# A gated recurrence stage, unrolled and skewed by one block over three engines

## The reference, cut to what matters

```python
h = layernorm(x)                      # rows of x, eps 1e-5
q, k, v, g = h @ Wq, h @ Wk, h @ Wv, h @ Wg
a = (h @ Wa)[:, :256] + 1j * (h @ Wa)[:, 256:]
a = sigmoid(abs(a)) * exp(1j * angle(a))
state[t] = a[t] * state[t - 1] + k[t] * v[t]   # complex, from 0 in each sequence
y = q * state                          # complex
y = groupnorm(y) * silu(g)             # groups of 8 channels, statistics over the sequence
```

## Time and profile before

| | |
|---|---|
| three runs, us | 3324.5, 3325.3, 3327.1; median 3325.3 |
| the profiled execution, us | 3331.5 |
| its span, us | 3329.7 |
| busy over the span | TensorE 80%, VectorE 59%, ScalarE 32%, GpSimd 41% |
| the stage that is changed | 0 to 395.5 us of the span |
| VectorE busy in it, us | 361.3 |
| granted clock of TensorE in it | 0.75 of 2.4 GHz; 0.90 from 620 us on |

### The profile page before, as it was taken

The page is one execution under the profiler, slowest core; times in us unless marked ns, Lnnn a source line. Parts: engine busy times, 40 slices in busy tenths (PEclk is TensorE's granted clock), DMA queues, the critical chain, the costliest instruction groups (busy, mean ns, idle before and its releaser), DMA issues. The chain is left out here.

```text
span 3329.7 us, 36467 instructions
## 1 busy us (share of the span) xinstructions
PE 2674.7 (80%) x12202; PEld 1820.2 (55%) x12202; DVE 1977.3 (59%) x3556; ACT 1053.3 (32%) x1637; POOL 1380.7 (41%) x865
## 2 busy tenths in 40 slices
PE   6555389956899999997477987879779676997998
PEld 2222156645799999996133433434334233665997
DVE  8999868645122222222788888999889894332111
ACT  4544222200111111111345545455454430221111
POOL 0000034426333333332058687686786852112332
PEclk8777699965899999998688998999889887998999
DMA  3000100011899999986200000101001000115996
GB/s 109 0 0 0 43 7 19 13 31 30 297 328 323 323 328 326 318 310 219 103 26 26 30 34 26 39 26 39 26 26 38 26 26 22 36 42 202 349 349 235
DMA packets 90565, 395.04 MB, mean 119 GB/s; under 512 B 20854, under 2 KB 48006, under 8 KB 63840
## 3 DMA queue, kind: packets, MB, share of 16 engines
q1 hardware_dynamic: 68864, 351.46, 30.0%
q0 software_dynamic: 21600, 42.37, 3.6%
HBM read 364.94 MB, written 39.29 MB: 121 GB/s over the span
## 5 line engine op out<-in xcount | busy, mean ns | idle before, releaser
L1240 POOL TENSOR_TENSOR ss_h<-ss_h,ss_cs 128x2048 f32<-128x2048 f32 x128 | 578.9, 4524 | 84.4 <-DVE ss_h L1603 76.6
L1320 PE MATMUL ss_y<-ss_h,all_ident 128*128 128x512 f32 x1024 | 528.3, 665 | 39.0 <-POOL ss_h L1240 39.0
L1095 DVE TENSOR_TENSOR experts_in<-experts_sil,experts_pU 128x512 f32<-128x512 f32 x176 | 121.0, 687 | 638.7 <-PE experts_pU L1039 638.7
L1603 DVE TENSOR_TENSOR_SCAN ss_h<-ss_da,ss_c_h,ss_dbu 128x512 f32<-128x512 f32 x384 | 470.7, 1268 | 38.9 <-ACT ss_da L1460 32.2
L1320 PEld LDWEIGHTS ss_y<-ss_h,all_ident 128*128 128x128 f32 x1024 | 216.8, 215 | 316.1 <-issue 266.6
L1460 ACT ACTIVATE ss_da<-ss_dt,ss_decay 128x512 f32<-128x512 f32 x512 | 326.5, 711 | 152.8 <-POOL ss_dt L1220 94.0
L1596 DVE TENSOR_TENSOR ss_dbu<-ss_dtx,ss_bB 128x1024 f32<-128x1024 f32 x256 | 314.5, 1229 | 62.2 <-PE ss_bB L1310 34.2
L1039 PE MATMUL experts_pG<-experts_xt,experts_wa 128*128 128x128 f32 x2816 | 346.7, 277 | 2.5 <-DMA experts_wa<-in_w_all 1.9
L1039 PE MATMUL experts_pU<-experts_xt,experts_wa 128*128 128x128 f32 x2816 | 344.2, 275 | 0.0
L1039 PEld LDWEIGHTS experts_pG<-experts_xt,experts_wa 128*128 128x128 f32 x2816 | 331.6, 193 | 3.6 <-issue 2.6
L1048 PE MATMUL experts_pY<-experts_wa,experts_in 128*128 128x256 f32 x1408 | 332.7, 379 | 0.0
(11 more groups left out here) (322 smaller groups left out, 3794.7 us busy)
## 6 DMA issues: line engine op xcount, KB each, us to landing
experts_wa<-in_w_all SPq DMA_DIRECT2D x176, 1536.0 KB, 9.1
ss_cs<-ss_c_rows SPq DMA_DIRECT2D x32, 1024.0 KB, 4.6
moe_rows<-route_xn SPq DMA_DIRECT2D x16, 512.0 KB, 3.1
all_x<-in_x SPq DMA_DIRECT2D x8, 512.0 KB, 9.2
gf_xb<-in_x SPq DMA_DIRECT2D x8, 512.0 KB, 3.8
ss_h<-moe_ys SPq DMA_DIRECT2D x4, 1024.0 KB, 6.9
moe_rows<-all_x SPq DMA_DIRECT2D x8, 512.0 KB, 3.3
experts_xr<-moe_rows,moe_token POOLq DMA_INDIRECT x176, 7.7
```

The lines of the kernel that those rows point to most:

```text
L1095: nc.vector.tensor_tensor(IN[t.two][:].rearrange("p f t -> p (f t)"), SIL[t.two][:], pU[t.two][:], ALU.mult)\
L1240: pool.tensor_tensor(h[:], h[:], CS[q % 2][:, n % GROUP].unsqueeze(1).to_broadcast([P, CI, BT]), ALU.mult)\
L1320: mm = pe.matmul(y[:, c], ident[:], H[n % RING][:, c], start=(n == 0), stop=(n == N - 1))
L1603: ins = V.tensor_tensor_scan(H[n % RING][:, c], DA[n % 2][:, c], DBU[:, c % 2], first, ALU.mult, ALU.add)
```

## The change

The hardware loops are gone on all three engines: eight blocks of straight code, with waits on constants. On VectorE and ScalarE the work is skewed by one block: in pass i VectorE does the half tangent of block i, the states of block i-1, the phase of block i, the inputs of block i+1 (K times V, magnitude squared, sign), and the outputs of block i-1. ScalarE interleaves likewise.

- The state's scans are multiplied by q at once (E1, E2), before the rotation back. The squares with their sums are taken of E1 and E2 on ScalarE (`sum_squares`), into pT, as |y|^2 is the same before and after the rotation. The real output keeps its order with three instructions; the imaginary one is only summed, its two products into two separate sums (SUMS and SUMX), added at the end.
- `normalise` and SGN go to ScalarE; normalise is one activation per 256 values with scale and bias per partition, in place in XN, one block further ahead. XNB and its copy back are gone.
- AR is copied by ScalarE (ARS), which frees the bank; the sign is taken from that copy. Its absolute value is taken from it later.
- The carries are read from the last column of the scans themselves (WR, UR, UI) or are 0 at a sequence's start.
- KV, QS, SN and CS have two buffers. A stays single: `decay(i)` waits for `scan_done` of the block before. MAG shares SQR, TAN shares SQI.
- 44 semaphores rather than 39.

The diff, cut to its core, its indentation shortened and calls joined on a line:

```diff
@@ buffers @@
-        keep = m_.sb("keep", [P, NB + 1])
-        c_phase, c_u = m_.sb("c_phase", [P, KD]), m_.sb("c_u", [P, KD, 2])
+        A = m_.sb("a", [P, KD, BT])
+        KV, QS, SN, CS = two("kv"), two("qs"), two("sn"), two("cs")
+        TA, TB = m_.sb("ta", [P, BT]), m_.sb("tb", [P, BT])
+        MAG, TAN = SQR, SQI
...
@@ TensorE: turn and project @@
+    wait(pe, "xt_done", i * KD)
+    wait(pe, "squared", (i - 2) * KD * 2)
...
-with pe.Fori(0, NB - 1) as i:
+pe.wait_ge(s["w_loaded"], 16)
+for i in range(NB):
     project(i)
-    turn(i + 1)
-project(NB - 1)
+    if i < NB - 1:
+        turn(i + 1)
@@ ScalarE @@
+def normalise(i):
+    act.wait_ge(s["stats_ready"], 1 if i == 0 else 2)
+    for t in range(i * TPB, (i + 1) * TPB):
+        A_(XN[:, t], XN[:, t], ACT.Identity, scale=rstd[:, t:t + 1], bias=shift[:, t:t + 1]).then_inc(s["xn_done"], 1)
 def copy_xt(i):
     act.wait_ge(s["xt_raw"], i + 1)
+    if i > 0:
+        act.wait_ge(proj[G_], i * KD)
...
+def squares(i):
+    wait(act, "t_done", i * KD)
+    wait(act, "atan_done", i * KD)
+    wait(act, "a_done", i * KD)
     for c in range(KD):
         act.wait_ge(proj[AR], i * KD + (c + 1))
         A_(SQR[:, c], bank_of(AR, c), ACT.Square)
-        A_(ABR[:, c], bank_of(AR, c), ACT.Abs)
+        A_(ARS[:, c], bank_of(AR, c), ACT.Copy).then_inc(free_of(AR, c), 1)
...
+def copy_q(i):
+    wait(act, "u_done", (i - 1) * KD)
...
+def magnitude(i):
+    wait(act, "turn_done", i * KD)
+    for c in range(KD):
+        act.wait_ge(s["neg_done"], i * KD + (c + 1))
+        A_(SGN[:, c], NEG[:, c], ACT.Copy, scale=-4.0 / math.pi, bias=1.0 / math.pi).then_inc(s["sgn_done"], 1)
+        A_(ARS[:, c], ARS[:, c], ACT.Abs)
     for c in range(KD):
         act.wait_ge(s["m2_done"], i * KD + (c + 1))
         A_(MAG[:, c], SQR[:, c], ACT.Sqrt).then_inc(s["mag_done"], 1)
+def decay(i):
+    wait(act, "scan_done", i * KD)
     for c in range(KD):
         act.wait_ge(s["mag_done"], i * KD + (c + 1))
-        A_(A[:, c], MAG[:, c], ACT.Sigmoid)
+        A_(A[:, c], MAG[:, c], ACT.Sigmoid).then_inc(s["a_done"], 1)
...
+def rotation(i):
+    wait(act, "y_done", (i - 1) * KD)
...
+def sum_squares(i):
+    act.wait_ge(s["xt_done"], min(i + 3, NB) * KD)
+    for c in range(KD):
+        act.wait_ge(s["u_done"], i * KD + (c + 1))
+        for n, src in ((2, E1), (3, E2)):
+            wait(act, "squared", (i * KD + c) * 2 + n - 3)
+            A_(pT[:, n - 2], src[:, c], ACT.Square, accum_out=sum_at(i, c, n)).then_inc(s["squared"], 1)
+normalise(0), copy_xt(0), squares(0), copy_k(0), normalise(1), copy_q(0), magnitude(0)   # one call a line
+for i in range(NB + 1):
+    more = i < NB - 1
+    if more: copy_xt(i + 1)
+    if i < NB - 2: normalise(i + 2)
+    if i < NB: angle(i); decay(i)
+    if more: squares(i + 1); copy_k(i + 1)
+    if i > 0: sum_squares(i - 1)
+    if i < NB: rotation(i)
+    if more: copy_q(i + 1); magnitude(i + 1)
@@ VectorE @@
+def inputs(i):                          # K times V, SQR + SQI, NEG from ARS
...
+def half_tangent(i):                    # waits for mag_done; every step waits for the one before
...
+def phase(i):                           # waits for atan_done, sgn_done; as before, without the copy of the carry
...
+        first = 0.0 if starts_at(i) else WR[:, c, BT - 1:BT]
...
+def states(i):
+    kv, qs, sn, cs = (b[i % 2] for b in (KV, QS, SN, CS))
+    for c in range(KD):
...
+        ch.mark(V.tensor_tensor(E1[:, c], kv[:, c], cs[:, c], ALU.mult))
+        last = ch.mark(V.tensor_tensor(E2[:, c], kv[:, c], sn[:, c], ALU.mult))
+    ch.wait(last)
+    dve.wait_ge(s["a_done"], i * KD + KD)
+    for c in range(KD):
+        for u, e in ((UR, E1), (UI, E2)):
+            first = 0.0 if starts_at(i) else u[:, c, BT - 1:BT]
+            last = V.tensor_tensor_scan(u[:, c], A[:, c], e[:, c], first, ALU.mult, ALU.add)
...
+        last.then_inc(s["scan_done"], 1)
...
+    for c in range(KD):
+        ch.mark(V.tensor_tensor(E1[:, c], qs[:, c], UR[:, c], ALU.mult))
+        V.tensor_tensor(E2[:, c], qs[:, c], UI[:, c], ALU.mult).then_inc(s["u_done"], 1)
+def outputs(i):
...
+    for c in range(KD):
+        ch.mark(V.tensor_tensor(ys_of(i, c), cs[:, c], E1[:, c], ALU.mult))
+        ch.link(V.tensor_tensor(TA[:], sn[:, c], E2[:, c], ALU.mult))
+        ch.link(V.scalar_tensor_tensor(ys_of(i, c), ys_of(i, c), 1.0, TA[:], ALU.mult, ALU.add, accum_out=sum_at(i, c, 0)))
+        ch.mark(V.scalar_tensor_tensor(TB[:], sn[:, c], 1.0, E1[:, c], ALU.mult, ALU.mult, accum_out=sum_at(i, c, 1)))
+        V.scalar_tensor_tensor(TA[:], cs[:, c], -1.0, E2[:, c], ALU.mult, ALU.mult, accum_out=...).then_inc(s["y_done"], 1)
...
+for i in range(NB + 1):
+    if i < NB: half_tangent(i)
+    if i > 0: states(i - 1)
+    if i < NB: phase(i)
+    if i < NB - 1: inputs(i + 1)
+    if i > 0: outputs(i - 1)
```

More of the change, by code:

```diff
@@ L264, in body @@
+                normalise(0)
+                copy_xt(0)
+                squares(0)
+                copy_k(0)
+                normalise(1)
+                copy_q(0)
+                magnitude(0)
+                for i in range(NB + 1):
+                    more = i < NB - 1
                     if more:
                         copy_xt(i + 1)
[L267 to L270, removed]
+                    if i < NB - 2:
+                        normalise(i + 2)
+                    if i < NB:
+                        angle(i)
+                        decay(i)
+                    if more:
+                        squares(i + 1)
+                        copy_k(i + 1)
+                    if i > 0:
+                        sum_squares(i - 1)
+                    if i < NB:
+                        rotation(i)
+                    if more:
+                        copy_q(i + 1)
+                        magnitude(i + 1)
@@ L284, in row_stats @@
                     norm_stats(nc, pre, lambda j: x_tile(a + j), stats[:, a:b], mv[:, a:b], rstd[:, a:b], tmp[:, a:b], 1e-5)
[L285 to L298, removed]
+                    V.scalar_tensor_tensor(shift[:, a:b], mv[:, a:b, 0], -1.0, rstd[:, a:b], ALU.mult, ALU.mult).then_inc(s["stats_ready"], 1)
+                ch = Chain(dve, s["steps"])
+                def inputs(i):
+                    for c in range(KD):
+                        dve.wait_ge(proj[V_], i * KD + (c + 1))
+                        wait_freed(dve, i, K_, c)
+                        V.tensor_tensor(KV[i % 2][:, c], KS[:, c], bank_of(V_, c), ALU.mult).then_inc(free_of(V_, c), 1)
                     for c in range(KD):
@@ new lines, in phase @@
+                def phase(i):
+                    dve.wait_ge(s["sgn_done"], i * KD + KD)
+                    wait(dve, "trig_done", i * KD)
+                    for c in range(KD):
+                        dve.wait_ge(s["atan_done"], i * KD + (c + 1))
+                        ch.link(V.tensor_tensor(TA[:], PHI[:, c], SGN[:, c], ALU.mult))
+                        first = 0.0 if starts_at(i) else WR[:, c, BT - 1:BT]
+                        ch.link(V.tensor_tensor_scan(PHI[:, c], TA[:], NEG[:, c], first, ALU.add, ALU.add))
+                        ch.link(V.tensor_scalar(TB[:], PHI[:, c], ROUND, ROUND, ALU.add, ALU.subtract))
+                        V.tensor_tensor(WR[:, c], PHI[:, c], TB[:], ALU.subtract).then_inc(s["turn_done"], 1)
+                        dve.wait_ge(s["turn_done"], i * KD + (c + 1))
@@ L363, in _ @@
                 row_stats(0, TPB)
-                normalise(0)
                 row_stats(TPB, NT)
                 dve.wait_ge(s["zeroed"], 32 * len(routes))
-                squares(0)
-                with dve.Fori(0, NB - 1) as i:
-                    body(i, True)
-                body(NB - 1, False)
+                inputs(0)
+                for i in range(NB + 1):
+                    if i < NB:
+                        half_tangent(i)
+                    if i > 0:
+                        states(i - 1)
+                    if i < NB:
+                        phase(i)
+                    if i < NB - 1:
+                        inputs(i + 1)
+                    if i > 0:
+                        outputs(i - 1)
@@ L371, in gate_loop @@
+                second = SUMS[:].rearrange("p (n f) -> p n f", f=4)[:, :, 1]
+                V.tensor_tensor(second, second, SUMX[:], ALU.add)
         m_.clear()
```

147 lines of the change are left out of this document (61 added, 86 removed).

## The result

The changed kernel takes 3287.9 us (median of four, 3285.2 to 3290.6) against 3326.2: ratio 0.9885, 95% interval 0.9868 to 0.9903. The forecast was 3280 and a gain of 45; it gained 38. VectorE's idle time stands where the forecast put it, ahead of the half tangent, but the ring through ScalarE is 1.1 us longer per block than forecast. In this ring the scans free A, ScalarE works from the sigmoid to the root, and VectorE's next half tangent needs the root.

The account below looks back on a forecast made before the run. The prediction took a ring through ScalarE to bound the changed kernel: six rings of 37.4 us from 72.8, then the last passes, end VectorE at 346.7 instead of 392.27; 45.3 less gives 3280 us, range 3266 to 3296.

Parts of the forecast that it names:

- the ring: ScalarE's work from the scans freeing A to the root VectorE's next half tangent needs: 37.4 us per block.
- VectorE's program per block: VectorE's instructions for one block after the change, summed start to start: 35.78 us against 45.70 before.
- The scans' end: On VectorE, the states' scans end 17.0 us after the start of half_tangent, letting the waiting sigmoids go.
- half_tangent(1): End of the pipeline's fill on VectorE: block 1's half tangent starts at 72.8 us, six rings following.
- half_tangent(0): First half tangent on VectorE, in the fill: starts at 44.0 us; the fill costs 10.
- copy_q: ScalarE's four instructions in the ring, 0.49 us each: 1.95 us per block, no table load counted.
- three per block rather than four: ScalarE's table loads per block, two of them in the ring, for sine and Sqrt: 1.41 us each, twice 2.8.
- The four sums: sum_squares on ScalarE, four accumulating instructions each waiting for the one before: 0.75 us each, 3.0 (2.6 to 3.4).
- A: Rival, chance 0.20: VectorE bounds after all, the ring being 1 or 2 shorter; 35.8 us per block, 3270 us.
- B: Rival, chance 0.22: longer ring from dear accumulations, late banks and small delays between engines; 39.8 us per block, 3294 us.
- C: Rival, chance 0.03: slower than before, TensorE never leaves 1.2 GHz; 46.9 us per block, 3373 us.
- D: Rival, chance 0.05: the longer straight program costs instruction fetches, or the edit does less than it says; 3300 to 3330 us.

Follow-up runs that it names:

- e3: The changed kernel with magnitude(i+1) ahead of copy_q(i+1) on ScalarE, in the prologue too: 3263.7 us, ratio 0.9813 to the kernel before.
- e4: The changed kernel with two buffers for A, K copied straight into KV, so decay no longer waits for the previous block's scans: 3273.7 us, ratio 0.9841.
- e2: The changed kernel with the four squares and their sums per block taken on VectorE again, A still single: 3294.2 us, ratio 0.9898.
- e5: The changed kernel with the first chunk of copy_q(i+1) ahead of rotation(i) on ScalarE: 3305.0 us on the slower chip, ratio 0.9878.
- e6: The changed kernel with two buffers for A and the squares with their sums on VectorE: 3315.2 us on the slower chip, ratio 0.9909.
- e8: The changed kernel run again without edits, on the slower chip: 3308.5 us, ratio 0.9892 to the kernel before.
- e1: The kernel before with its three hardware loops of gate_loop written out, nothing else: 3318.0 us against 3326.3, ratio 0.9979.
- e7: The changed kernel with two buffers for A, magnitude ahead of copy_q and another order in the first two blocks: 3278.8 us on the slower chip, ratio 0.9800.

## Why the prediction was right, and where it was off

The mechanism held: VectorE's program per block was forecast at 35.78, and where nothing stops it (e3, e4) it takes 35.81. The ring over `decay`, squares, rotation and magnitude is what the changed kernel runs at: e3 and e4, at different places, made it shorter than VectorE's program. The scans' end came at 17.05 for 17.05, half_tangent(1) at 73.7 for 72.8, half_tangent(0) at 43.96 for 44.0. So close a hit on the last is in part luck: in e2, e4, e5, e6 and e8, whose edits leave what comes before it nearly untouched, it came at 43.87 to 45.23.

The gain was 37.1 in the stage for 45.3. The term of the sum that was mis-sized is the ring, by the number of its table loads: it has three and not two, a block four and not three. Term by term from 129.11:

| term | forecast | measured |
|---|---|---|
| sigmoids | 1.19 | 1.32 |
| squares, copy_k with its wait | 5.46 | 5.45 |
| sum_squares | 3.0 | 2.44 |
| rotation with the sine's load | 4.5 | 4.74 |
| copy_q | 1.95 | 3.33 |
| magnitude to the load | 2.1 | 2.20 |
| load and root | 2.06 | 2.05 |

The prediction has "three per block rather than four", with one load for the sine and one for Sqrt in the ring, and puts the one for silu at nothing without giving a reason. In the kernel before, one load served silu and the sines behind it. The change turns their order round: sine first, and the table loaded for it isn't one that silu can use. I had looked at which functions shared a table, not at which came first. That costs 1.38. The four sums, taken at 0.75 and measured at 0.61, gave 0.56 back, so a second error hid part of the first; small differences in the other terms took the rest. At 38.5 instead of 37.4, six blocks late by 1.1 each, 0.9 in the fill, 0.5 in the last passes and 0.2 more for the semaphores make the 8.2.

The price of a load itself was taken from the row, and rightly: 143.65 to 144.94 is 1.29, and so are 138.96 to 140.25 and 148.59 to 149.88. Nor is there time ahead of a load: the copy at 143.06 lasts 0.57, until 143.63. The Trainium skill, page "ScalarE: Activation LUTs", section What ACT_TABLE_LOAD costs, states 2.66 for a switch; these loads disagree. By its figure, as an estimate, the ring with its three loads would be 38.5 + 3 x 1.37 = 42.6, and 38.5 was measured.

Of the rivals, A (VectorE bounds) is what e3 and e4 make true. B (a ring of 39.8) pointed the right way, by another cause: its dear accumulations were cheap. C did not happen: K1's products begin at 1.2 GHz as forecast, after a stop of 4.72 (5.9 forecast), but all it cost was the 0.44 ahead of copy_k (0.5 forecast). G1 was early enough: TensorE was through with the block's products at 144.3, and ScalarE read G1 at 145.91. D is refuted by e1, and by the 35.81 of e3 and e4, which is the forecast program without any loss.

What the parts are worth, by stage ends: unrolling 10.9 (e1). The remaining 26.2 come from the moved and saved VectorE work, less the fill and the ring. The ring withholds 16.4 (e4), the order in the fill another 14 (e7 against e4). Parts other than the unrolling and the squares (normalise, SGN, the carries, the products around q) were not undone singly, so what each is worth is not shown.

## What to carry to other kernels

Taking work off the busiest engine pays until the first wait on a single buffer closes a ring through the other engine; before moving anything, follow that engine's program from the wait to what the busiest engine needs next, and put the work that nobody waits for behind that point. When functions of several tables are reordered, count the loads again in the new order. A pipeline's filling has its own critical path, and the order that is right for the steady blocks may be wrong for the first two.

## What the runs showed of the hardware

- One table served silu and the sines where silu came first, and not where the sine came first: the sine's line has one load in e5 and eight in the changed kernel, silu's line eight in both.
- From a load's start to the start of the activation behind it are 1.29 to 1.30, between activations that otherwise start 0.5 apart (e5: 139.43 to 140.73).
- The hardware loop cost this program 1.56 of a block of 45.70 (e1: 44.14 without it).
- An activation that sums its output is followed by a read of 0.19, yet four of them, each waiting for the last, start 0.61 apart, where the absolute value and the sine of the rotation (141.40 and 141.92), without a wait or a sum, start 0.52 apart: sum and wait together cost under 0.1.
- Two chips differed by 20 us (0.6%) on the same kernel, 3326.3 and 3346.6 for the one before. The changed one took 3287.9 where the one before took 3326.2, and 3308.5 on the slower chip. For the changed one all of the difference lies outside the stage studied, whose ends agree within 0.2 us (358.46 and 358.26).
